# The opening of a twelve-block decoder in one block, with ScalarE making the rectified gates and TensorE subtracting the rounded parts

## The reference

```python
f_gate = x_t * w_f
i_gate = x_t * w_i
hidden = x_t * w_h
diff = softplus(-f_gate) - softplus(-i_gate)
log_f = -softplus(diff)
log_i = -softplus(-diff)
log_values = log_i + log_g(hidden)      # g: hidden + 0.5 above zero, sigmoid(hidden) below
h_t = parallel_scan_log(log_f, log_values)
```

## Time and profile before

| | us |
|---|---|
| median of three runs | 2594.25 |
| lowest, highest | 2590.24, 2604.8 |
| profiled execution, its own time | 2600.38 |
| span in the profile, first to last instruction | 2598.6 |
| end of the set-up block's last work | 11.2 |
| end of the opening's last instruction | 108.87 |

### The profile page before, as it was taken

One profiled execution on the slowest core, in us unless ns is written; L12 is line 12 of the kernel. 1 busy time (PEld: TensorE's weight loads), 2 busy tenths in 40 slices (PEclk: granted clock), 3 DMA queues, 4 the chain that ended last, 5 costly groups with the idle time before them and its releaser, 6 DMA issues. The chain is left out here.

```text
span 2598.6 us, 41898 instructions
## 1 busy us (share of the span) xinstructions
PE 2276.5 (88%) x15210; PEld 1512.3 (58%) x15210; DVE 1431.6 (55%) x3533; ACT 1125.8 (43%) x1923; POOL 659.1 (25%) x868
## 2 busy tenths in 40 slices
PE   1489999998889999949999998799998798699996
PEld 1387754444436699934444444367665545589995
DVE  6825366785565221158999965666566555511114
ACT  6533335655433011134777774421443334234444
POOL 6110132222110133322011012000356310245551
PEclk8689978988998999966999999789999898699998
DMA  5200122330112189933222101031111210689996
GB/s 195 64 5 1 27 48 46 50 50 18 30 34 106 39 309 334 329 108 54 34 41 35 26 7 46 2 91 58 33 27 19 57 18 2 217 293 354 355 343 235
DMA packets 86208, 268.89 MB, mean 103 GB/s; under 512 B 25306, under 2 KB 43858, under 8 KB 69740
## 3 DMA queue, kind: packets, MB, share of 16 engines
q1 hardware_dynamic: 70324, 233.10, 29.4%
q0 software_dynamic: 15680, 33.12, 4.0%
HBM read 207.36 MB, written 23.94 MB: 89 GB/s over the span
## 5 line engine op out<-in xcount | busy, mean ns | idle before, releaser
L1616 ACT ACTIVATE prob<-st_ps 128x1024 f32<-128x1024 f32 x448 | 412.9, 933 | 220.0 <-PE st_ps L1483 218.7
L1636 DVE TENSOR_REDUCE cmax<-ring 128x1 f32<-128x512 f32 x640 | 401.2, 682 | 43.7 <-PE ring L1491 41.4
L3082 PE MATMUL A<-xbT,w 128*128 128x128 f32 x2512 | 301.3, 276 | 0.3 <-issue 0.3
L3082 PEld LDWEIGHTS A<-xbT,w 128*128 128x128 f32 x2512 | 291.4, 193 | 0.8 <-issue 0.5
L1530 PE MATMUL acc<-prob,v 128*32 128x256 f32 (+2 forms) x3200 | 267.0, 408 | 13.4 <-DVE byq L1674 12.3
L3326 DVE COPY yb<-C 128x256 f32<-128x256 f32 x118 | 50.1, 425 | 283.7 <-PE C L3090 277.5
L2999 POOL DMA_INDIRECT y_rows_dram<-yb,dst x118 | 116.4, 986 | 323.8 <-DVE yb L3326 320.7
L3090 PE MATMUL C<-w,hid 128*128 128x256 f32 x632 | 149.5, 380 | 0.0
L1483 PE MATMUL st_ps<-qst,kst 64*128 64x512 f32 (+3 forms) x560 | 137.3, 489 | 7.3 <-DMA qst<-parts 3.1
L2986 POOL DMA_INDIRECT xb<-x_rows_dram,src x118 | 115.1, 976 | 99.9 <-DVE src L3296 64.6
L1632 DVE CUSTOM_DVE_ANT_0 masked<-ring,causal_wide 128x512 bf16<-128x512 f32 (+3 forms) x256 | 112.5, 487 | 47.8 <-PE ring L1491 46.9
(11 more groups left out here) (475 smaller groups left out, 4491.7 us busy)
## 6 DMA issues: line engine op xcount, KB each, us to landing
w<-L3f_W_dram SPq DMA_DIRECT2D x79, 1026.0 KB
w<-L1f_W_dram SPq DMA_DIRECT2D x39, 1536.0 KB
room<-y_rows_dram SPq DMA_DIRECT2D x8, 1024.0 KB, 10.4
kst<-parts SPq DMA_DIRECT2D x120, 64.0 KB, 2.4
qst<-parts SPq DMA_DIRECT2D x120, 64.0 KB, 2.4
gate<-L2f_gates_dram SPq DMA_DIRECT2D x5, 1536.0 KB, 7.1
first<-parts SPq DMA_DIRECT2D x96, 64.0 KB, 2.4
qT<-dense SPq DMA_DIRECT2D x84, 64.0 KB, 2.4
```

The costliest lines, as they stand in the source:

```text
L1616: act.activation(prob[:, step % PROBS, 2 * p:2 * p + 2, 0:n], st_ps[:, p, :, 0:n], ACT.Exp, scale=scale)\
L1636: dve.tensor_reduce(cmax[:, a, t:t + 1, k0 // CH], spot(key)[:, 0:k1 - k0], AX.X, ALU.max)\
L3082: mm = pe.matmul(A[:, j % 2 * 2 + a, f * TB:(f + 1) * TB], up_w(w[:, j % WB], a, k, f), xbT[:, j % 2, k, :], start=(k == 0), stop=(k == KT ...
```

## The change

`setup` is gone. `constants` makes the same tiles and loads as parts that the recurrence's block calls, with a second matrix `minus`, which has -1 on its diagonal. `ident` and `minus` come first on GpSimd. `xT` comes in four pieces, one for each item, and the masks later. On SP's queue `x` and `ctxT` move ahead of the reload of `down_rows`. ScalarE makes max(-v, 0) with Relu, for two items at a time, and the sigmoid of w_h x directly. g(hidden) becomes max(w_h x + 0.5, sigmoid(w_h x)). VectorE adds both softplus parts in one instruction, and `diff` has four buffers, in the room of `h_out`. TensorE adds -1 times the rounded part to the product that still stands in PSUM, and ScalarE copies the remainder as the `lo` part; the plain copies and GpSimd's subtractions go. The order of ScalarE's and VectorE's work is written out anew.

```diff
-def setup(nc, env, dram):
...
+def constants(nc, env, st, dram):
...
+    minus = sbuf(nc, st, "minus", [P, P])
+    def load_x(sp, i):
+        k, b = i // NB, i % NB
+        sp.dma_start(env.xT[:, k, b * S:(b + 1) * S], dram.xT[k * P:(k + 1) * P, b * S:(b + 1) * S]).then_inc(x_in[i], 16)
...
+    def run(pool):
+        for t in (env.ident, minus):
+            pool.memset(t[:, :], 0.0).then_inc(s.ident_cleared, 1)
...
@@ folding, load
-        down_coefs(0, 2)
-        up_coefs(0, 3)
+        begin.load_x(sp, 0)
+        down_coefs(0, 1)
+        up_coefs(0, 1)
+        begin.load_x(sp, 1)
+        down_coefs(1, 1)
+        up_coefs(1, 2)
         sp.dma_start(down_rows[:, :, :], dram["W_con"]).then_inc(s.down_loaded, 16)
+        begin.load_x(sp, 2)
+        begin.load_x(sp, 3)
         for i in range(3):
             down_coefs(2 + i, 1)
             up_coefs(3 + i, 1)
         sp.dma_start(up_rows[:, :, :], dram["W_expT"]).then_inc(s.up_loaded, 16)
         sp.dma_start(ups[:, 0, :], dram["up_bias"]).then_inc(s.up_bias_loaded, 16)
+        begin.load_pads(sp)
         down_coefs(STEPS, 2)
         sp.wait_ge(s.down_kept, 1)
         sp.dma_start(dram["fold_down"].rearrange("(p r) d -> p r d", p=P), down_rows[:, :, :]).then_inc(s.down_stored, 16)
         up_coefs(6, 4)
+        sp.dma_start(env.x[:, :, :], dram["x"].rearrange("(t p) d -> p t d", p=P)).then_inc(s.x_loaded, 16)
+        sp.dma_start(env.ctxT[:, :, :], dram["ctxT"].rearrange("(k p) t -> p k t", p=P)).then_inc(s.x_loaded, 16)
         sp.wait_ge(s.down_stored, 16)
         sp.dma_start(down_rows[:, :, :], dram["fold_down"].rearrange("(f n) d -> n f d", n=P)).then_inc(s.down_back, 16)
         down_coefs(STEPS + 2, STEPS - 2)
...
@@ folding, run
-        pool.wait_ge(s.con_kept, 2)
-        pool.tensor_tensor(fold.con_lo[:, :, :], down_rows[:, :, :], fold.con_hi[:, :, :].bitcast(F32), ALU.subtract)
...
@@ folding, products, after the second down and up products
+        pe.wait_ge(begin.minus_shaped, 1)
+        pe.wait_ge(s.con_high, 1)
+        for f in range(NB8):
+            mm = pe.matmul(A[:, f, :], begin.minus[:, :], fold.con_hi[:, f, :].bitcast(F32), start=False, stop=True, skip_group_check=True)
+        mm.then_inc(s.con_left, 1)
+        pe.wait_ge(s.con_low, 1)
         for r in range(NB8):
             mm = pe.matmul(A[:, 0, r:r + 1], spread[:, 1, r, :], up_rows[:, r, D:D + 1], start=True, stop=True)
         mm.then_inc(s.second_bias, 1)
+        pe.wait_ge(s.w_high, 1)
+        for k in range(KT):
+            for r in range(NB8):
+                mm = pe.matmul(up_w[:, k, r, :], begin.minus[:, :], high_w[:, k, r, :].bitcast(F32), start=False, stop=True, skip_group_check=True)
+        mm.then_inc(s.w_left, 1)
...
@@ min_gru, scalar
+                sides(0)
+                sides(1)
+                exponents(0)
+                exponents(1)
+                logs(0)
+                logs(1)
+                beside.first_down(act)
+                sides(2)
+                beside.first_up(act)
+                sides(3)
+                exponents(2)
+                exponents(3)
+                logs(2)
+                logs(3)
+                gates(0)
+                beside.down_high(act)
+                gates(1)
+                beside.down_low(act)
+                gates(2)
+                beside.up_high(act)
+                beside.second_bias(act)
+                gates(3)
+                beside.up_low(act)
...
@@ min_gru, vector
+                beside.chain(dve, 2)
+                hidden(0)
+                hidden(1)
+                soften(0)
+                soften(1)
+                begin.pads(dve)
+                beside.chain(dve, 3)
+                soften(2)
+                soften(3)
                 for n in range(len(items)):
                     if n >= 2:
-                        hidden(n - 2)
...
+                        dve.wait_ge(s.scanned, n - 1)
+                        hidden(n)
                     scan(n)
```

More of the change, by code:

```diff
@@ L530, in folding @@
                  "first_up first_bias second_up second_bias first_down second_down up_kept bias_kept bias_done down_kept "
-                 "up_stored up_back bias_stored bias_back down_stored down_back con_kept w_kept")
+                 "up_stored up_back bias_stored bias_back down_stored down_back con_high con_low con_left w_high w_low w_left x_loaded")
     u_ready = (s.coef_u0, s.coef_u1, s.coef_u2)
@@ L657, in products @@
         for f in range(NB8):
-            mm = pe.matmul(A[:, f, :], spread[:, 3, f, :], down_rows[:, f, :], start=True, stop=True)
+            mm = pe.matmul(A[:, f, :], spread[:, 3, f, :], down_rows[:, f, :], start=(f % 2 == 0), stop=True, skip_group_check=True)
         mm.then_inc(s.second_down, 1)
@@ L679, in keep_first_up, with keep_down_high, keep_down_low, keep_up_high @@
         act.activation(up_rows[:, :, D], A[:, 0, 0:NB8], ACT.Copy).then_inc(s.up_kept, 1)
[L681 removed]
+    def keep_down_high(act):
         act.wait_ge(s.second_down, 1)
[L683 to L686 removed]
+        act.activation(fold.con_hi[:, :, :], A[:, :, :], ACT.Copy).then_inc(s.con_high, 1)
+    def keep_down_low(act):
+        act.wait_ge(s.con_left, 1)
+        act.activation(fold.con_lo[:, :, :], A[:, :, :], ACT.Copy).then_inc(s.con_low, 1)
+    def keep_up_high(act):
+        act.wait_ge(s.second_up, 1)
+        act.activation(high_w, up_w, ACT.Copy).then_inc(s.w_high, 1)
+    def keep_up_low(act):
+        act.wait_ge(s.w_left, 1)
+        act.activation(low_w, up_w, ACT.Copy).then_inc(s.w_low, 1)
+    def keep_second_bias(act):
         act.wait_ge(s.second_bias, 1)
         act.activation(ups[:, 2, :], A[:, 0, 0:NB8], ACT.Copy).then_inc(s.bias_kept, 1)
[L689 to L698 removed]
+    return named(load=load, marks=marks, chain=chain, run=run, products=products, first_up=keep_first_up, first_down=keep_first_down,
+                 down_high=keep_down_high, down_low=keep_down_low, up_high=keep_up_high, up_low=keep_up_low, second_bias=keep_second_bias)
+def min_gru(nc, env, dram, weights, fold, ahead, first):
     with ExitStack() as st:
```

173 lines of the change are left out of this document (98 added, 75 removed).

## The result

| | before | after |
|---|---|---|
| median of 18 runs each, us | 2594.38 | 2579.2 |
| lowest to highest | 2588.86 to 2604.8 | 2574.02 to 2588.94 |
| profiled execution, its own time | 2600.38 | 2578.14 |
| span in the profile | 2598.6 | 2576.4 |
| end of the opening's last instruction | 108.87 | 97.88 |

The ratio of after to before is 0.9948, with a 95% interval of 0.9937 to 0.9959: 15.2 us by the medians, inside the stated range and within a few us of the point, 2582.0.

The account below looks back on a forecast made before the run. Transfers and GpSimd pace the opening's first half, VectorE the second. Chain 3 ends at 62.7, the hand-off tail at 96.6 instead of 108.87: -12.3 us from the median 2594.25 gives 2582.0 us, range 2569 to 2593.

Parts of the forecast that it names:

- Chain 3: Opening's third recurrence chain: VectorE stands 14 us for a queued down coefficient; ends at 62.7, against 64.60 before.
- VectorE's saving behind it: Opening after chain 3: VectorE has 28.4 us left instead of 44.3, alone ending at 91; possible gain 16 us.
- the relus are hidden: Opening, ScalarE: eight rectified gates, 8.3 us, covered by 9 us before the second down product.
- a hand-off chain: Opening's tail: TensorE and ScalarE alternate on products, remainders, copies and gates, from 62.7 to 96.6.
- w_left: Opening's tail, TensorE takes the rounded up part off, reading with a step of 8: 7.1 us, ending at 92.7.
- Rival A: SP's queue doesn't hold d7 back: chain 3 ends near 56, opening at 90, -19 us, 2575; chance 0.15.
- d7: Down coefficient needed by chain 3, queued behind x, ctxT and the down_rows reload; in at 55.6.
- Rival D: SP's queue from 42 to 56 bounds everything: 12 us more makes a loss, 38 us more gives 2608; chance 0.03.
- Rival B: Tail hand-offs cost more, +1.9 and +4.3 us on two remainder products: opening ends at 103, 2588; chance 0.2.
- the end of the first chain: Opening's first recurrence chain on VectorE: ends at 26.0 instead of 30.95, keeping 5 of 10.6 us head start.
- the wait for u9: SP's queue: last up coefficient waits for GpSimd's step 6, 9.5 us behind the down_rows store, at 42.8.
- The moved step: SP's queue: x and ctxT go ahead of the down_rows reload, issued at 43.1 and landed by 51.9.

Follow-up runs that it names:

- x_late: Changed kernel with the loads of x and ctxT issued only after the reload of up_rows; 2578.64 us, ratio to before 0.9933.
- d_first: Changed kernel with another queue order alone: chain 3's down coefficients ahead, x and ctxT last; 2567.48 us, ratio to before 0.9907.
- pool_lo: Changed kernel with remainders made as before: ScalarE copies both products twice, GpSimd subtracts, no minus matmuls; 2582.69 us, ratio to before 0.9942.
- relu_back: Changed kernel with the eight rectified gates made on VectorE again instead of ScalarE; 2583.68 us, ratio to before 0.9942.
- tail: Changed kernel with only the ScalarE and TensorE hand-offs reordered, up_hi and w_left in halves; 2568.06 us, ratio to before 0.9905.
- after_again: The changed kernel, unchanged, profiled a second time; 2584.01 us, ratio to before 0.9948.

## Why the prediction was right, and where its steps were off

**The form was right.** Chain 3 is held by the queue (`x_late`, `d_first`), VectorE's saving behind it comes for 9.5 us of 16.7 from passes without GpSimd over them (`pool_lo`), the relus are hidden (`relu_back`), and a hand-off chain with `w_left` and `up_low` ends last (`tail`). Rival A, a queue that lets d7 overtake, is refuted by the 16.23 us. Rival D would have needed 12 us more in that queue; d7 was in at 57.4 instead of 55.6, 1.8 us more. Rival B didn't come: of the 6.2 us that it put on `con_left` and `w_left`, `w_left` took 0.7 (7.82), and `con_left` none (3.62, as planned).

**Step by step**, in the first trace:

| step | predicted | after |
|---|---|---|
| third down coefficient used | 17.4 | 17.97 |
| end of chain 2 | 26.0 | 27.86 |
| store of `down_rows` | 33.3 | 36.22 |
| `x` issued | 43.1 | 44.87 |
| d7 used | 55.6 | 57.44 |
| end of chain 3 | 62.7 | 64.46 |
| end of the second down product | 68.3 | 69.63 |
| `con_high` done | 70.2 | 71.55 |
| `con_low` done | 78.6 | 79.42 |
| `up_high` done | 85.5 | 86.15 |
| `w_left` | 7.1 long, to 92.7 | 7.82 long, to 94.02 |
| `up_low` done | 96.6 | 97.88 |
| VectorE alone | 91 | 92.02 |

Two terms of the sum were mis-sized. The first is the end of the first chain: I took the spreading of before, 1.36 us, and it took 2.80. GpSimd's own spreading began 0.24 us earlier and ended at 26.78, and VectorE's ended 1.1 us behind it:

```profile
24.82 1.96 POOL L642 TENSOR_TENSOR spread<-small,spots 128x1024 f32<-128x1024 f32 x1
```

The product behind it took 6.28 us, and the store came 2.9 us late; the wait for u9 (from 36.22 to 44.87, 8.65 instead of 9.5) gave some of it back, and what was left came through `x` and d7 to the end of chain 3, 1.8 us late. The moved step itself was sized right: from the issue of `x` to d7 it was 12.57 us, and 12.5 were planned.

The first term is not the same in each execution. In `after_again` VectorE's spreading began first, and it was GpSimd's that was stretched:

```profile
23.80 1.63 DVE L642 TENSOR_TENSOR spread<-small,spots 128x1024 f32<-128x1024 f32 x1
```

```profile
24.43 2.76 POOL L642 TENSOR_TENSOR spread<-small,spots 128x1024 f32<-128x1024 f32 x1
```

There chain 2 ended at 25.43, chain 3 at 62.51 and the opening at 96.19, each within 0.6 us of the forecast. Which of the two engines starts first is decided by less than a microsecond; the forecast didn't have this branch, and that it came out so near in one trace is in part luck.

The second is `w_left`. I put 1.4 us for the step on top of the low clock's price, by a strided weight load; the rows don't fix that figure, and that it was near is luck. The two prices don't add: the step sets 244 ns an instruction at both clock levels, 7.82 us in each kernel that has the product in one piece, and the contiguous read is 5.82. My lower bound, 5.7, was right, the value taken 0.7 us short. On the other side the tail's second down product was 5.11 instead of 5.5. From the end of chain 3 to the end it was 33.4 us, and 33.9 were planned, so the errors inside the tail cancel, and the opening's 1.3 us over the forecast come from ahead of it.

**What the 11.0 us are made of.** Undone alone, the merged block is worth 4.4 us, the remainders on TensorE 3.3, the gates on ScalarE 0.4 (within the scatter), and the earlier place of `x` on the queue costs 4.6, part of it scatter. If these add, which no run tests, some 7 us are left for what was not undone by itself: the one maximum in place of three operations, the single addition for each softplus, and the new order of the work. The passes that are gone from VectorE behind chain 3 are of that size, but no run shows that they are the cause. Another order on the queue would have given 9.5 us on top, and 13.7 together with the order of the hand-offs.

**The medians.** 15.2 us and, in the second comparison, 10.3 (2594.35 and 2584.01) stand around the forecast of 12.3, as do the openings' 11.0 and 13.5. The rest of the first figure needs no cause in the change. The ratio of 0.9948 lies beside the border of half a per cent, as said.

**What stays open.** `tail` and `d_first` gained 26.5 and 27.1 us by their medians, against 2594.54 for the kernel before, measured beside them, while their openings are 17.6 and 21.2 us shorter than 109.92, the longer of the two. The 6 to 9 us beyond that lie behind the opening in their traces or in other runs of it, and `x_late` shows the opposite (14.1 by the medians, 15.6 to 16.4 in the opening). No run tells why.

## What to carry to other kernels

A large load that nobody needs yet should stand on a queue behind every small one that the next chain waits for: here 2 MB too early lengthened the wait for a 256 KB load from 9.8 to 16.2 us, and with the small loads first it was 1.3. When an engine is slow only at times, look for another engine's long pass at that very moment before counting its instructions; here two such meetings were 9.5 of the 16.7 us that VectorE saved behind chain 3. And when work goes from a saturated engine to a chain of hand-offs, write down the chain's own end at once: it becomes the bound, and its order is then the next thing to change.

## What the runs showed of the hardware

A moving operand of 128 fp32 columns read with a step of 8 elements costs 244 to 254 ns an instruction at the low clock and at the full one, 7.82 us for the product; the contiguous read in the same place went at some 6 instructions a microsecond at 0.50 and 11 at 0.98. So this strided read on TensorE was free at the low clock and cost nearly a factor of two at the full one. Where a two-input pass of VectorE and one of GpSimd meet, the one that begins later is stretched, as if it waited the other out: VectorE's 1.20 and 1.23 us became 5.50 and 6.42, each ending 1.1 us behind GpSimd's subtraction, and 0.42 became 2.00 under a spreading; but where VectorE's spreading began first, it took 1.63 and GpSimd's 2.76. And the same code behind the opening took 2478 to 2494 us, with a mean clock of the run that follows it.
